# A two-layer attention and mixture-of-experts kernel: mixing with tokens on partitions, raw rows to the experts, biases on TensorE

## The reference

```python
x = x + attn_a(layernorm(x), Wq, bq, Wk, bk, Wv, bv)     # softmax(q k^T / sqrt(8)) v in blocks of 64
x = x + ffn(layernorm(x), Wr, Wg, Wu, Wd)
x = x + attn_b(layernorm(x), w_tor, b_tor, in_proj_w, in_proj_b, out_w, out_b)
x = x + ffn(layernorm(x), Wr, Wg, Wu, Wd)

def ffn(x):                                    # 8 experts, hidden 512, the best 2 of each token
    logits = x @ Wr
    top_vals, top_idx = top_k(logits, 2)
    combine = sum(softmax(top_vals)[..., None] * one_hot(top_idx, 8), axis=1)
    h = silu(x @ Wg[e]) * (x @ Wu[e])
    return einsum('ne,nec->nc', combine, (h @ Wd[e]) / sqrt(12))
```

## Time and profile before

| | us |
|---|---|
| median of 3 runs | 976.49 |
| lowest, highest | 972.31, 977.88 |
| the profiled execution | 975.18 |
| its span, first to last instruction | 973.4 |

### The profile page before, as it was taken

The page is one execution under the profiler, slowest core; times in us unless marked ns, Lnnn a source line. Parts: engine busy times, 40 slices in busy tenths (PEclk is TensorE's granted clock), DMA queues, the critical chain, the costliest instruction groups (busy, mean ns, idle before and its releaser), DMA issues. The chain is left out here.

```text
span 973.4 us, 26881 instructions
## 1 busy us (share of the span) xinstructions
PE 708.4 (73%) x8764; PEld 583.4 (60%) x8765; DVE 523.4 (54%) x1810; ACT 473.5 (49%) x876; POOL 396.2 (41%) x458
## 2 busy tenths in 40 slices
PE   1688877831699999998077898761109999999940
PEld 1356555521588888887035676661108888888830
DVE  3367888863356555554253565642305555555524
ACT  0689877630355555553058897520005555555510
POOL 1223777786033333333231154588732333333320
PEclk9989999975799999999558999985559999999985
DMA  7001222212111111111330000001211111111107
GB/s 204 8 12 45 68 83 87 76 56 67 32 47 47 49 46 47 47 47 36 99 118 24 26 3 10 31 29 39 69 39 41 49 44 49 47 47 49 45 20 259
DMA packets 54045, 54.51 MB, mean 56 GB/s; under 512 B 8272, under 2 KB 43472, under 8 KB 53968
## 3 DMA queue, kind: packets, MB, share of 16 engines
q1 hardware_dynamic: 42608, 32.19, 12.1%
q0 software_dynamic: 8704, 18.11, 5.8%
q10 hardware_dynamic: 2656, 3.15, 0.9%
HBM read 29.51 MB, written 23.90 MB: 55 GB/s over the span
## 5 line engine op out<-in xcount | busy, mean ns | idle before, releaser
L1581 POOL DMA_INDIRECT expert_out<-moe_a_out,moe_a_place x72 | 69.0, 958 | 153.0 <-DVE moe_a_out L1716 153.0
L1581 POOL DMA_INDIRECT expert_out<-moe_b_out,moe_b_place x72 | 69.0, 958 | 152.7 <-DVE moe_b_out L1716 152.7
L1613 PE MATMUL wide<-wgu,moe_a_hi 128*128 x288 | 96.7, 417 | 0.5 <-issue 0.5
L1613 PE MATMUL wide<-wgu,moe_b_hi 128*128 x288 | 96.7, 417 | 0.4 <-issue 0.4
L1629 PE MATMUL wide<-wd,moe_a_hidT 128*128 x576 | 76.4, 276 | 1.1 <-DVE moe_a_out L1716 0.7
L1629 PE MATMUL wide<-wd,moe_b_hidT 128*128 x576 | 76.4, 276 | 1.0 <-DVE moe_b_out L1716 0.7
L1669 ACT ACTIVATE moe_a_glow<-wide 128x512 f32<-128x512 f32 x72 | 43.0, 598 | 69.9 <-PE wide L1613 69.8
L1669 ACT ACTIVATE moe_b_glow<-wide 128x512 f32<-128x512 f32 x72 | 43.0, 598 | 69.6 <-PE wide L1613 69.5
L441 POOL DMA_INDIRECT routed<-la_norm_x,la_place x64 | 63.6, 994 | 23.0 <-issue 19.3
L1629 PEld LDWEIGHTS wide<-wd,moe_a_hidT 128*128 128x128 f32 x576 | 70.0, 192 | 1.7 <-issue 1.7
L1629 PEld LDWEIGHTS wide<-wd,moe_b_hidT 128*128 128x128 f32 x576 | 70.0, 192 | 1.6 <-issue 1.6
(11 more groups left out here) (257 smaller groups left out, 1693.4 us busy)
## 6 DMA issues: line engine op xcount, KB each, us to landing
moe_a_rows<-routed SPq DMA_DIRECT2D x72, 66.0 KB, 1.9
moe_b_rows<-routed SPq DMA_DIRECT2D x72, 66.0 KB, 1.9
lb_outs<-expert_out SPq DMA_DIRECT2D x8, 512.0 KB
la_stage<-in_wg SPq DMA_DIRECT2D x8, 256.0 KB, 2.6
la_stage<-in_wu SPq DMA_DIRECT2D x8, 256.0 KB, 2.8
wd<-in_wd SPq DMA_DIRECT2D x8, 256.0 KB, 3.7
kept<-stream SPq DMA_DIRECT2D x8, 256.0 KB, 3.6
stream<-kept SPq DMA_DIRECT2D x8, 256.0 KB
```

Source lines behind the costliest of these rows:

```text
L1581: pool.indirect_dma_start(d.expert[:, :], bass.IndirectOffsetOnAxis(ap=place[s % 4][:, 0:1], axis=0), out[u][:, :], None).then_inc(stored[ ...
L1613: last = nc.tensor.matmul(ps[u][:, :], x[u][:, :], w(j, part), start=i == 0, stop=i == 2)
```

## The change

- `mixing`: probT is loaded as weights, `stand` moves through; the result has tokens on partitions. `flip`, `out_side`, `side` and the memset of psO go; `divide` reads the result directly. In the second layer `mix` gets two buffers.
- The biases: bias_values and bias_out go from POOL. In `setup` each bias row is split into three bf16 parts in rows 0, 32 and 64 of `k.offset`; PE adds them by a bf16 matmul with ones ahead of `project_v` (first layer, two matmuls of 512 columns) and `map_out` (second layer, one).
- Rows are sent raw: `k.stream` has six more columns, with token, expert, weights, and the reciprocal root and its product with the negated mean (`root2` writes these). `norm_x` and `normalise2` go. Each expert step normalises its rows on ACT (`normalise`), three steps ahead. The logits come from raw rows: Wr gets its mean removed in `setup`, and `take` multiplies by the root.
- The routing stands nearer: second layer measure2, turn_x2 c-2, logits c-3, ranks c-4, dispatch c-4 and c-5; in the first layer logits and ranks come half a quad sooner, and both use PSUM bank psP[1].
- PE's, DVE's and ACT's lists are put in a new order; the first layer's weights are split two pieces a pair in pairs 0 to 7.

```diff
+            for layer, offset in enumerate(k.offset):
+                for j in range(3):
+                    nc.vector.tensor_copy(offset[32 * j:32 * j + 1, :], part[32 * j:32 * j + 1, j, layer, :])
...
+                rows = k.stream[:, c * BATCH:(c + 1) * BATCH, :]
+                nc.gpsimd.tensor_scalar(root_in2[u][:, 0, :], mom2[u][:, :, 1], EPS, None, ALU.add)
+                nc.gpsimd.tensor_scalar(root_in2[u][:, 1, :], mom2[u][:, :, 0], -1.0, None, ALU.mult).then_inc(part_rooted2, 1)
+                pool.wait_ge(part_rooted2, 2 * c + 1)
+                nc.gpsimd.tensor_tensor(rows[:, :, D + 4], root_in2[u][:, 0, :], k.const[:, C_ROOT:C_TOKEN].to_broadcast([P, BATCH]),
+                                        ALU.pow).then_inc(part_rooted2, 1)
+                pool.wait_ge(part_rooted2, 2 * c + 2)
+                nc.gpsimd.tensor_tensor(rows[:, :, D + 5], root_in2[u][:, 1, :], rows[:, :, D + 4], ALU.mult).then_inc(rooted2, 1)
...
-                    if 0 <= c - 1 < QUADS:
-                        root2(c - 1)
-                if 0 <= p - 2 < 2 * EXPERTS:
-                    weight_low(p - 2)
+                if 0 <= p < EXPERTS:
+                    weight_low(2 * p)
+                    weight_low(2 * p + 1)
...
+                for cls in range(2):
+                    nc.tensor.matmul(psX[BLK * cls:BLK * (cls + 1), :], k.ones[:, 0:BLK],
+                                     k.offset[0][:, cls * 64:(cls + 1) * 64].unsqueeze(1).to_broadcast([P, 2 * BATCH, 64]),
+                                     start=True, stop=False, tile_position=(0, BLK * cls))
...
-                        for b in range(2):
-                            for i in range(4):
-                                col = t * 256 + gp * P + b * BLK
+                        for i in range(4):
+                            for b in range(2):
+                                col = ((2 * t + gp) * 4 + i) * 2 * (HD + 1)
                                 last = nc.tensor.matmul(
-                                    psO[32 * i:32 * i + 2 * (HD + 1), col:col + BLK],
-                                    stand[c % 2][:, p % 2 * 2 + t, b, 4 * gp + i, :],
-                                    probT[p % 2][gp][t][:, i * P + b * BLK:i * P + (b + 1) * BLK], start=True, stop=True,
-                                    tile_position=(0, 32 * i))
+                                    psO[BLK * b:BLK * (b + 1), col:col + 2 * (HD + 1)],
+                                    probT[p % 2][gp][t][:, i * P + b * BLK:i * P + (b + 1) * BLK],
+                                    stand[c % 2][:, p % 2 * 2 + t, b, 4 * gp + i, :], start=True, stop=True,
+                                    tile_position=(0, BLK * b))
...
-                if ahead:
-                    score(p + 1, 0)
-                if even and 0 <= c - 3 < QUADS:
-                    route_ranks(c - 3)
                 if behind:
                     mixing(p - 1)
                 if even and 0 <= c + 1 < QUADS:
                     project_k(c + 1)
-                if not even and 0 <= c - 2 < QUADS:
-                    route_logits(c - 2)
+                if ahead:
+                    score(p + 1, 0)
+                if even and 0 <= c - 2 < QUADS:
+                    turn_x2(c - 2)
                 if here:
                     turn(p, 0, 0)
                     turn(p, 0, 1)
-                if ahead:
-                    score(p + 1, 1)
-                if behind:
-                    flip(p - 1)
                 if even and 0 <= c + 1 < QUADS:
                     project_q(c + 1)
                 if not even and 0 <= c + 1 < QUADS:
                     project_v(c + 1)
+                if ahead:
+                    score(p + 1, 1)
                 if here:
                     turn(p, 1, 0)
                     turn(p, 1, 1)
                 if even and 0 <= c - 2 < QUADS:
-                    turn_x2(c - 2)
+                    route_logits(c - 2)
+                if not even and 0 <= c - 2 < QUADS:
+                    route_ranks(c - 2)
...
+            def take(c):
+                dve.wait_ge(logits, c + 1)
+                dve.wait_ge(rooted2, c + 1)
+                scale = k.stream[:, c * BATCH:(c + 1) * BATCH, D + 4:D + 5]
+                nc.vector.tensor_tensor(logit[:, :, :], psP[1][:, 0:BATCH * EXPERTS].rearrange("p (t e) -> p t e", e=EXPERTS),
+                                        scale.to_broadcast([P, BATCH, EXPERTS]), ALU.mult).then_inc(taken, 1)
...
                     peak(p, 0)
                     shift(p, 0)
-                if 0 <= p - 2 < PAIRS:
-                    divide(p - 2)
                 if even and 0 <= c - 3 < QUADS:
-                    weigh(c - 3)
-                    spots(c - 3)
-                if even and 0 <= c - 2 < QUADS:
-                    normalise2(c - 2)
+                    spot_ranks(c - 3)
+                if not even and 0 <= c - 2 < QUADS:
+                    take(c - 2)
                 if here:
                     peak(p, 1)
                     shift(p, 1)
-                if even and 0 <= c + 2 < QUADS:
-                    measure1(c + 2)
+                if 0 <= p - 1 < PAIRS:
+                    divide(p - 1)
+                if even and 0 <= c - 3 < QUADS:
+                    weigh(c - 3)
+                    find_places(c - 3)
                 if not even and 0 <= c - 2 < QUADS:
                     route(c - 2)
                     count(c - 2)
+                if even and 0 <= c + 2 < QUADS:
+                    measure1(c + 2)
                 if not even and 0 <= c - 1 < QUADS:
                     measure2(c - 1)
...
+            for c in range(-3, QUADS + 5):
+                if 0 <= c - 3 < QUADS:
+                    root2(c - 3)
+                if 0 <= c - 5 < QUADS:
+                    dispatch((c - 5) * BATCH + 2)
+                    dispatch((c - 5) * BATCH + 3)
                 if 0 <= c + 3 < QUADS:
                     root1(c + 3)
-                if 0 <= c + 2 < QUADS:
-                    bias_out(c + 2)
-                for t in range((c - 6) * BATCH, (c - 6) * BATCH + 2):
-                    if 0 <= t < TILES:
-                        dispatch(t)
-                if 0 <= c - 3 < QUADS:
-                    root2(c - 3)
-                    normalise2(c - 3)
-                for t in range((c - 6) * BATCH + 2, (c - 6) * BATCH + 4):
-                    if 0 <= t < TILES:
-                        dispatch(t)
+                if 0 <= c - 4 < QUADS:
+                    dispatch((c - 4) * BATCH)
+                    dispatch((c - 4) * BATCH + 1)
...
+                    if c >= 3:
+                        pe.wait_ge(taken, c - 2)
                     elif c >= 1:
                         pe.wait_ge(flat_copied, 4 * c)
                 elif w == 0:
                     if c >= 2:
-                        pe.wait_ge(back_copied, c - 1)
+                        pe.wait_ge(summed, c - 1)
                     else:
                         pe.wait_ge(flat_copied, 4 * c + 1)
-                elif c >= 4:
-                    pe.wait_ge(taken, c - 3)
                 else:
                     pe.wait_ge(flat_copied, 4 * c + 2)
...
+                nc.tensor.matmul(psP[0].rearrange("p (t c) -> p t c", c=D), k.ones[:, :],
+                                 k.offset[1][:, :].unsqueeze(1).to_broadcast([P, BATCH, D]), start=True, stop=False)
...
+            for c in range(-3, QUADS + 5):
                 here, ahead, behind = 0 <= c < QUADS, 0 <= c + 1 < QUADS, 0 <= c - 1 < QUADS
+                if 0 <= c - 4 < QUADS:
+                    route_ranks(c - 4)
+                if 0 <= c - 3 < QUADS:
+                    route_logits(c - 3)
+                if behind:
+                    mixing(c - 1, 0)
                 if ahead:
                     score(c + 1, 0)
-                if 0 <= c - 5 < QUADS:
-                    route_ranks(c - 5)
-                if behind:
-                    mixing(c - 1, 0)
                 if here:
                     turn(c, 0, 0)
                     turn(c, 0, 1)
                 if 0 <= c + 2 < QUADS:
                     project_k(c + 2)
-                if behind:
-                    flip(c - 1, 0)
                 if 0 <= c - 2 < QUADS:
                     turn_back(c - 2)
-                if 0 <= c - 4 < QUADS:
-                    route_logits(c - 4)
+                if behind:
+                    mixing(c - 1, 1)
                 if ahead:
                     score(c + 1, 1)
-                if behind:
-                    mixing(c - 1, 1)
-                if 0 <= c + 2 < QUADS:
-                    project_q(c + 2)
+                if 0 <= c - 2 < QUADS:
+                    map_out(c - 2)
                 if here:
                     turn(c, 1, 0)
                     turn(c, 1, 1)
-                if 0 <= c - 2 < QUADS:
-                    map_out(c - 2)
+                if 0 <= c + 2 < QUADS:
+                    project_q(c + 2)
                 if ahead:
```

(53 more changed lines are left out.)

417 lines of the change are left out of this document (189 added, 228 removed).

## The result

The changed kernel is slower: 991.87 us against 976.7, a ratio of 1.0188 [1.0127, 1.0249]. The forecast was 933.5 us, so 58 us are missing. Its profiled execution took 991.78 us, span 990.0.

What follows compares the result with a forecast made beforehand. Experts were taken as PE-bound, the attention layers as waits between engines, the second layer's end as POOL's dispatch. Terms -29.5 - 8 - 3 - 3 + 1.1 + 0.2 = -42.2 gave 933.5 us; 917 to 953 was to hold some 0.83.

Steps and rivals of the forecast that it cites:

- Part 2: Mixing turned over: 2.15 us each in the first layer (1.1 more), 0.65 in the second (0.6 less); flip and copy go.
- Part 3: First layer's period: quads of 20.2 us against 21.8, PE and ACT in turn being the loop; 8 us saved.
- Part 5: Second layer's period: 16.4 us an iteration against 17.15, the loop on ACT; 3 us saved, bounds -8 and +8.
- The sign that was to be read from `take`: First layer, DVE: quads near 20.2 us without a wait of `take` would show the forecast right.
- Rival (a): Turned mixing's weight loads don't overlap: 3.7 us in the first layer, 1.85 in the second; about 961 us; chance 0.06.
- Part 1: POOL in the second layer: 28 dispatches done before the last shift, three normalisations fewer behind it; 29.5 us saved.
- Part 4: First layer's tail, taken as bound by POOL: two weight pieces leave it, 2.5 us; 3 us saved.
- Part 6: Experts: an Identity of 0.41 us per step in ACT's idle gap, only each stage's start pays; 1.1 us lost.
- (b): In-order waits eat the periods: root1 late +10 us, add_map late +6; 950 us; chance 0.12.
- (d): First layer's mixing at 1.0 us, its period set by DVE; 922 us; chance 0.12.
- (e): Change doesn't do what it says: places come a quad late, 16 dispatches less early; 953 us; chance 0.03.
- (c): Experts: ACT's Identity waits for its load and holds back `glow` and PE; slower than before, 990 us; chance 0.03.

Runs made afterwards that it cites:

- j2: Changed kernel with 54-column mixing and useless matmuls in PE's waits, first layer only; usual-speed chip: 975.6 us, ratio 0.9994 to the kernel before.
- j1: Changed kernel with first-layer 54-column mixing and useless matmuls, second-layer ranks and logits behind the first score, useless matmuls there too; usual-speed chip: 963.8 us, ratio 0.986.
- e2: Changed kernel with the first layer's logits moved from ahead of the mixing to behind the odd pair's first score: 997.9 us, ratio 1.023.
- e3: Changed kernel with two useless 512-column matmuls (ballast) ahead of each first-layer mixing: 994.4 us, ratio 1.016.
- g2: Changed kernel with four useless 512-column matmuls ahead of each first-layer mixing: 1016.8 us, ratio 1.043.
- g3: Same kernel as e3, two useless matmuls ahead of each first-layer mixing, run again on another chip: 1004.9 us, ratio 1.029.
- g4: Kernel before with POOL relieved in the second layer alone (normalise2 on DVE, dispatch five quads behind instead of six): 960.1 us, ratio 0.983.
- e1: Changed kernel with the first layer's mixing back in its former orientation, flip and copy included, new PE order kept: median 1018.5 us, ratio 1.033.
- f1: Changed kernel, unchanged, on the slower chip: 1050.5 us, ratio 1.0236.
- f2: Same kernel as j1, on the slower chip: 1032.3 us, ratio 1.0033.

## Why the prediction was wrong, point by point

**The step that failed** is none of the terms by itself. It is that every duration of Parts 2, 3 and 5 was taken at the full clock, and that PE's clock was not among the things that the change could move. The kernel before had it at 0.98 and 0.97 in the steady stretches; the changed one at 0.83 and 0.80. Summed over stretches of half a microsecond, from the first peak to pair 14 and to c7, the low-clock time rises from 6.8 + 3.4 + 18.5 + 3.4 = 32 to 1.9 + 40.1 + 29.5 + 23.9 = 95 us, 63 more, 32 of lost work by the estimate of halves: more than half of the missing 58. The experiments took less than that back. j2 shows it for the first layer in runs of its own: with the clock held, 16 us come back although work is added. j1, which also changes the second layer, gives 28 of the 58. The other 30 are in part low clock that is left (17 us of it from c4 to c7 in j1) and in part open.

**Part 3, first layer's period.** Forecast 20.2 us, measured 24.5. Less the lost work, with the 40.1 us summed above, (122.3 - 20.1) / 5 = 20.4 us. e2, e3, g2 and g3 give 21.1, 21.5, 22.2 and 21.3 by the same working, of which 0, 0.9, 1.7 and 0.9 are ballast. The chain of work was summed up nearly rightly, the clock under it was not. Two things qualify this. The kernel before comes to 21.45 us by the same working, not 21.8, so at a like clock the change is worth 1.0 us a quad and not 1.6. And j1 and j2, whose clock is at full without any working, take 21.4 a quad, useless work included. The sign that was to be read from `take` failed on its own: it was to wait no more, and waits 4.7 to 5.5 us in each quad, 25.7 in five where the copy in its place waited 10.4 before:

```profile
168.45 0.19 DVE L710 TENSOR_TENSOR la_logit<-wide,stream 128x32 f32<-128x32 f32 x1 [4.72 <-PE wide L538]
168.56 1.21 DVE L683 TENSOR_REDUCE la_most<-wide 128x16 f32<-128x1024 f32 x1
```

The peak behind it has had its score since 165.4. j1 has this wait too, 4.7 us a quad at full clock; whether it costs the period anything was not tried. The quads at either end were put at nothing and cost 3.0 and 2.8 us; the weight copies at twice the rate stand in the first ones, but that was not tried.

**Part 2, mixing.** Forecast 2.15 and 0.65 us. Measured at full clock 2.05, and 0.77 in the second layer:

```profile
618.57 0.77 PE L1169 MATMUL wide<-lb_stand,lb_probT 128*32 128x36 f32 x64
```

The next row starts 0.70 us later, the spacing that the forecast counted. Right, and the neighbours in `project_v` were the right rows. Rival (a) was the Trainium skill's rule on overlapping loads, "TensorE: Matmul & The Clock Gate", section "The mechanism": an estimate by it is over 4 us for 64 loads of 64 columns. The trace disagrees again, with 32 ns each. What I left out is the other side of the turning: the same 64 instructions now move 18 columns each instead of 64, so that 2 us in which PE is "busy" do little.

**Part 5, second layer's period.** Forecast 16.4, measured 20.4; less the lost work (61.18 - 12.0) / 3 = 16.4. But the kernel before comes to (51.45 - 1.7) / 3 = 16.6 by the same working: its 17.15 held low clock too, and at a like clock the new order is worth 0.2 us an iteration, not 0.75. The 12.2 us up to c4 were not forecast; 5.5 of them are half of the low-clock time that came there (29.5 against 18.5), the rest is open.

**Part 1, POOL in the second layer.** Forecast -29.5, measured -29.7 up to the experts. 26 dispatches lie ahead of the last shift's end instead of 28, and the last one ends 55.8 us behind it, not 56.8. The mechanism is right, and that the number fits to 0.2 us is partly luck: two more dispatches, 2.5 us, were left behind the last shift, while POOL worked on instead of standing till +6 us, with 1.2 us idle. It waits for `place` 4.5 us in all. g4 shows the mechanism alone: 20 us in the tail.

**Part 4, first layer's tail.** Forecast -3, measured +1.9. The step that failed is "POOL bounds this one too": the first dispatches of the last two quads wait 7.4 and 6.2 us for `place`, at 208 and 228 us, where they waited 1.1 and 0.4 before. PE falls to its lower level 1.5 us ahead of the last shift's end here (214.7 and 216.2 us), and fell to it 11 us behind that in the kernel before (207.3 and 196.0). In j1, with no fall ahead of the tail, it is 12 us behind again; there and in j2 the second of these waits is 2.4 us, and from the last shift's end to the last dispatch's it takes 41.2 us, against 43.6 before and 44.9 in the changed kernel: most of the forecast's gain.

**Part 6, experts.** The Identity takes 0.49 us and not 0.41. It took as long before: the forecast's 0.41 is a quarter of a row of four that overlap (1.65 us), each of them 0.48 or 0.49 us long. It lies in ACT's gap as said, and the gap ahead of `glow` shrinks from 0.98 to 0.6. The step stays at 2.83 us:

```profile
399.14 0.49 ACT L1633 ACTIVATE moe_a_rows<-moe_a_rows 128x128 f32<-128x128 f32 x1
400.23 0.60 ACT L1652 ACTIVATE moe_a_glow<-wide 128x512 f32<-128x512 f32 x1 [0.60 <-PE wide L1587]
```

**The rivals.** (b), (d) and (e) were variants of the waits and are not what happened: no wait for root1 shows in the changed kernel, and PE's 0.9 us an iteration for `add_map` lie within the 16.4 that Part 5 came to. (b)'s wait for root1 does appear in e1, 2.7 us. (c) did not come. (a)'s loads do overlap. The true one was missing. The signs were few but there: the earlier trace rows has 8s inside the layers, and the earlier trace rows 0.92 in the stretch that I took as steady; I read them as facts of the stage and never as a thing that PE's own order and the columns it moves can bring on. The range was built from bounds of durations alone. The order whose fewer waits I counted as a gain also puts ranks, logits and mixings in a row.

The Trainium skill, "TensorE: Matmul & The Clock Gate", section "HAM oscillation — how this bites in real kernels", tells of a kernel that falls to the lower clock in each turn of its loop while PE waits for a transfer. Here too the clock falls about once in each turn of the loop, but not over a transfer: the longest wait of PE in these quads is 1.41 us, the longest right ahead of a fall 0.91, and the rest of the stretch is work that the profile counts as busy.

**Open.** Wide mixing alone and fillers alone were run on the slower chip only. The changed kernel was not run on the chip of j1 and j2. What of logits, mixing and wait is the least that must be filled is not known, nor why falls come in one execution of a kernel and not in another (e3 and g3, on two chips). Some 30 of the missing 58 us came back in no run; `take`'s wait and the 12 us up to c4 are where I would look.

## What to carry to other kernels

Sum up a PE-bound loop at the clock that it will have, not at the one that it had: look for places where instructions that move few columns come to stand in a row or behind a wait, and price such a place at about half of the low-clock time per turn. And take the old period at a like clock, or its low clock is counted as a gain of the new order. Here fewer moved columns in as many instructions saved nothing and stood where the clock fell; useless wide matmuls in the waits together with a wider mixing paid 16 us in the first layer (j2), and in the second layer showed no gain over the better order. The part that held alone was the one read from a queue that never waits: POOL's relief in the kernel before gives 960.1 us (g4), the shortest time of the study, though on another chip than j1's 963.8 and with overlapping intervals.

## What the runs showed of the hardware

A mixing with 54 moved columns takes 2.08 us where one with 18 takes 2.05: with 64 columns loaded at two positions the moved ones are free up to there. One and the same kernel (e3, g3) had 19 and 44 us at the lower clock in one stretch on two chips, 116.7 and 128.1 us long. And chips differ by 5%: on one the kernel before took 1026 us, and in the first layer's stretch of f1 the waits named "issue" ahead of PE's instructions came to 5.3 us, in f2 to 6.7, where the traces of the same kernels on the chips of the usual speed have none.
